# Gathering every second expert tile by quarters of a row and turning it on VectorE in squares of 32

## What is computed

```python
def _L0_ffn_ref(x, gate_W, gate_b, W1, b1, g1, be1, W2, b2, g2, be2):
    xf = x.reshape(BN, D)                       # 4096 x 512, already normalised
    gate_scores = xf @ gate_W + gate_b
    topk_scores, topk_idx = jax.lax.top_k(gate_scores, 2)
    weights = jax.nn.softmax(topk_scores, axis=-1)
    def expert(w1, bb1, gg1, bbe1, w2, bb2, gg2, bbe2):
        h = jax.nn.relu(_layernorm(xf @ w1 + bb1, gg1, bbe1))
        return _layernorm(h @ w2 + bb2, gg2, bbe2)
    all_out = jax.vmap(expert)(W1, b1, g1, be1, W2, b2, g2, be2)
    exp_out = all_out[topk_idx, jnp.arange(BN)[:, None]]
    return (jnp.sum(weights[..., None] * exp_out, axis=1) + xf).reshape(B, N, D)
```

## Time and profile before

| | |
|---|---|
| median of 3 runs | 1172.0 us (1169.74 to 1174.47) |
| profiled execution | 1170.26 us, its span 1168.5 us |
| granted TensorE clock, mean | 0.991 |
| busy: PE, PEld, DVE | 95%, 77%, 78% of the span |
| busy: ACT, POOL | 62%, 34% |
| DMA, mean | 124 GB/s |

### The profile page before, as it was taken

How to read it: one execution, slowest core, us unless ns; L and a number is a source line. 1 busy time by engine, 2 the same in 40 slices (tenths; PEclk the granted TensorE clock), 3 DMA queues, 4 the chain that set the end, 5 groups by cost and what they waited for, 6 DMA issues and landing times.

```text
span 1168.5 us, 24237 instructions
## 1 busy us (share of the span) xinstructions
PE 1108.3 (95%) x6017; PEld 905.0 (77%) x6018; DVE 910.5 (78%) x2172; ACT 722.2 (62%) x2148; POOL 393.4 (34%) x328
## 2 busy tenths in 40 slices
PE   6999999999989999999999888999999999999993
PEld 5888888888877787777777666777888888888882
DVE  6888888887874778878878877877777777777774
ACT  5223332233377777768676644866787787877873
POOL 3000000000034433545536364445534434443432
PEclk9999999999999999999999998999999999999998
DMA  8544545445340133143143377786555454444543
GB/s 261 163 149 159 190 148 173 151 163 207 126 147 1 57 89 111 56 124 100 46 145 90 128 206 219 201 249 152 94 85 81 81 85 80 86 81 81 88 63 40
DMA packets 95316, 144.76 MB, mean 124 GB/s; under 512 B 20864, under 2 KB 37428, under 8 KB 94607
## 3 DMA queue, kind: packets, MB, share of 16 engines
q1 hardware_dynamic: 77338, 106.83, 28.8%
q0 software_dynamic: 17216, 35.73, 17.4%
q10 hardware_dynamic: 693, 1.36, 0.4%
HBM read 82.69 MB, written 64.76 MB: 126 GB/s over the span
## 4 chain that ended last, share of the span: by engine, by line
PE 72%; DVE 9%; issue 7%; DMA 6%; ACT 3%; POOL 2%; DVEq 0%; POOLq 0%; ACTq 0%; SPq 0%
PE banks L1126 27%; PE banks L716 17%; PE banks L928 7%; PE banks L781 6%; DMA out<-rows,scatter_rows 4%; PE banks L893 3%; PE banks L906 3%; PE banks L1154 2%; PE banks L1138 2%; ACT rows L1335 2%; DVE operands L1615 2%; PE banks L917 1%; PE banks L754 1%; DVE rows L1917 1%; ACT operands L1218 1%
## 5 line engine op out<-in xcount | busy, mean ns | idle before, releaser
L1126 PE MATMUL banks<-operands 128*128 x1608 | 390.5, 398 | 9.2 <-ACT operands L1218 5.0
L1126 PEld LDWEIGHTS banks<-operands 128*128 128x128 f32 x1608 | 299.5, 190 | 73.9 <-issue 14.2
L716 PE MATMUL banks<-operands 128*128 128x512 f32 (+2 forms) x1224 | 290.1, 393 | 3.6 <-DVE operands L1615 3.6
L716 PEld LDWEIGHTS banks<-operands 128*128 128x128 f32 (+1 forms) x1224 | 226.1, 192 | 48.3 <-DVE operands L1615 3.7
L1218 ACT ACTIVATE operands<-banks 128x512 fp32r<-128x512 f32 (+1 forms) x232 | 137.6, 602 | 63.4 <-PE banks L807 34.2
L1615 DVE TENSOR_TENSOR operands<-banks,operands 128x512 fp32r<-128x512 f32 (+1 forms) x232 | 156.7, 683 | 15.6 <-ACT operands L1218 12.2
L1335 ACT ACTIVATE rows<-banks,score_shift 128x77 f32<-128x77 f32 x512 | 158.4, 337 | 11.2 <-DVE score_shift L1839 10.9
L2686 POOL DMA_INDIRECT out<-rows,scatter_rows x67 | 106.4, 1588 | 155.3 <-DVE rows L2419 109.7
L1218 ACT ACTIVATE operands<-rows 128x512 fp32r<-128x512 f32 (+2 forms) x77 | 54.0, 710 | 163.6 <-DVE rows L1686 139.4
L1540 ACT ACTIVATE banks<-banks,param_cols 128x128 f32<-128x128 f32 x268 | 99.2, 431 | 82.2 <-PE banks L1154 75.6
L2357 DVE BATCH_NORM_STATS2 moe_stats<-banks 128x6 f32<-128x512 f32 x134 | 93.2, 696 | 37.5 <-PE banks L1126 31.5
(11 more groups left out here) (191 smaller groups left out, 1603.1 us busy)
## 6 DMA issues: line engine op xcount, KB each, us to landing
expert_parts<-operands SPq DMA_DIRECT2D x32, 512.0 KB, 3.0
operands<-expert_parts SPq DMA_DIRECT2D x8, 2048.0 KB, 11.4
rows<-in_x SPq DMA_DIRECT2D x8, 1024.0 KB, 5.5
rows<-in_L_ffn_W SPq DMA_DIRECT2D x32, 256.0 KB, 3.6
x_rows<-rows SPq DMA_DIRECT2D x8, 1024.0 KB, 4.3
rows<-x_rows SPq DMA_DIRECT2D x8, 1024.0 KB, 6.2
xf_rows<-rows SPq DMA_DIRECT2D x32, 256.0 KB
out<-rows SPq DMA_DIRECT2D x32, 256.0 KB
```

Of the source, the lines that this page charges most:

```text
L716: last = nc.tensor.matmul(dst, stationary(a, k), moving(b, k), start=(t == 0 and k == 0), stop=(t == len(terms) - 1 and k == n_k - 1))
L1126: last = nc.tensor.matmul(dst, stationary[:, a, k, :], weights[:, w, bass.ds(e, 1), a2, k, :].rearrange("p e f -> p (e f)"), start=False, ...
```

## The change

The 27 tiles of even number from 14 on (`in_squares`) take another way from the table to xT:

- Their rows are read as four quarters of 128 features. An index now names a quarter of a row: token x 4 + quarter. Partition 32q + r of the buffer gets quarter q of four tokens, in four indirect DMAs of 128 pieces of 512 bytes. The first two go in GpSimd's turn of tile i-5, the other two in that of tile i-4.
- VectorE turns the buffer in 32x32 squares (`turn_rows`) at the start of the turn of tile i-3, from buffer `xg[0]` into `xq_turned` in SBUF. TensorE's four transposes of these tiles are gone. `rows_hi` and `rows_lo` read xq_turned.
- For the squares to come out with features on partitions, partition p holds features 4p to 4p+3. So W1's rows are loaded in that order for all tiles, and the transposes that stay on TensorE read every fourth element of the gathered rows.
- Each of these tiles has its slots loaded a second time in four pieces, one for each group of 32 partitions (`square_slots`), and the index is made by a scalar_tensor_tensor instead of a copy.
- In the turns with a `turn_rows`, ScalarE's square root goes behind the high part of the hidden rows.
- One semaphore for the transposed rows becomes two, and one wait at the start moves to another semaphore.

```diff
+SQUARES_FROM = 14
+SQUARES_N = SQUARES_FROM // 2
+        xf_quarters = xf_d.rearrange("t (q f) -> (t q) f", q=KC)
+        xq_rows = xg[0].rearrange("p (b f k) -> p b k f", b=P // SQ, k=KC)
+        xq_turned = f_at(60, KC * P)
+        xq_features = xq_turned.rearrange("p (k b r) -> p k r b", k=KC, b=P // SQ)
...
+        def in_squares(n, u):
+            return u == 0 and (not isinstance(n, int) or n >= SQUARES_N)
...
-                    src = io[name].rearrange("e (k p) f -> e k p f", p=P)
+                    src = io[name].rearrange("e (k p) f -> e k p f" if n // 2 else "e (p k) f -> e k p f", p=P)
...
+                if in_squares(n, u):
+                    for q in range(KC):
+                        sp.dma_start(square_slots[q * SQ:(q + 1) * SQ, bass.ds(n - SQUARES_N, 1)].rearrange(
+                            "p n b w -> p (n b w)"), slots_d[bass.ds(row, P), :].rearrange(
+                                "(r b) w -> r (b w)", r=SQ)).then_inc(slots_in[u], 16)
...
-                    last = nc.tensor.transpose(cx_bank[u][:, k * P:(k + 1) * P], xg[u][:, k * P:(k + 1) * P], ident[:, :])
-                last.then_inc(cx_done, 1)
+                    last = nc.tensor.transpose(cx_bank[u][:, k * P:(k + 1) * P],
+                                               xg[u].rearrange("p (f k) -> p k f", k=KC)[:, k], ident[:, :])
+                last.then_inc(cx_done[u], 1)
...
-                if after >= 3:
+                if after >= 3 and not in_squares(n + 1 + u, 1 - u):
                     rows_in(n + 1 + u, 1 - u)
...
+                if in_squares(n, u):
+                    hi_part(xT[:, HI].rearrange("p k (r b) -> p k r b", r=SQ), xq_features).then_inc(cx_hi, 1)
+                else:
+                    hi_part(xT[:, HI].rearrange("p k t -> p (k t)"), cx_bank[u]).then_inc(cx_hi, 1)
...
-                if after is not None and after >= 2:
+                if after is not None and after >= 2 and not behind:
                     deviations(i, True, True)
                 need(act, m2_done, i)
                 act.wait_ge(relu_done, KC * (i + 1))
                 hi_part(hTc[:, HI].rearrange("p k t -> p (k t)"), ch_bank).then_inc(hh_ready, 1)
+                if after is not None and after >= 2 and behind:
+                    deviations(i, True, True)
...
                 rows = slice(q * SQ, (q + 1) * SQ)
+                V.memset(quarter_ix[rows, 0, :], float(q))
...
+            def turn_rows(n):
+                dve.wait_ge(gathered[0], gathers(n + 1, 0))
+                need(dve, cx_lo, 2 * n - 1)
+                V.transpose(xq_turned.rearrange("p (k b r) -> p b k r", k=KC, r=SQ), xq_rows).then_inc(cx_done[0], 1)
...
+                if in_squares(n, u):
+                    V.scalar_tensor_tensor(
+                        gix_squares, square_slots[:, bass.ds(n - SQUARES_N, 1), :, 0].rearrange("p n b -> p (n b)"),
+                        float(KC), quarter, ALU.mult, ALU.add).then_inc(gix_ready, 1)
+                    return
...
+                if after >= 3 and in_squares(n + 1 + u, 1 - u):
+                    turn_rows(n + 1 + u)
...
+                if in_squares(n, u):
+                    for b in parts:
+                        G.indirect_dma_start(xg[0][:, b * P:(b + 1) * P], None, xf_quarters,
+                                             bass.IndirectOffsetOnAxis(gix_squares[:, b:b + 1], 0)).then_inc(
+                            gathered[u], 16)
+                    return
...
-                if after >= 5:
+                if u == 0 and after >= 4 and in_squares(n + 2, 0):
+                    gather(n + 2, 0, (2, 3))
+                if after >= 5 and in_squares(n + 2 + u, 1 - u):
+                    gather(n + 2 + u, 1 - u, (0, 1))
+                elif after >= 5:
                     gather(n + 2 + u, 1 - u)
```

75 lines of the change are left out of this document (44 added, 31 removed).

## The result

The change makes the kernel slower: 1194.0 us (median of 4 runs, 1191.7 to 1196.8) against 1172.2 in the same sitting, a ratio of 1.0194 with the 95% interval 1.017 to 1.0217. The profiled execution has a span of 1191.2 us for 1168.5. The forecast of 1166.0 and its range to 1177 are both missed.

What follows compares the result with a forecast made beforehand. The prediction took TensorE to bound the kernel. From the profiled 1170.3 us, -11.7 for removed transposes, +3.5 and +2.5 at the start and +1.5 for the later expert load gave 1166.0 us, range 1159 to 1177.

Steps and rivals of the forecast that it cites:

- worth 0.43 us: TensorE: removing one group of row transposes saves 0.43 us, 27 times, -11.7 us if nothing else comes to bind.
- Four transfers for one: GpSimd, steady part: the extra gathers add 3.9 us per two tiles, 10.3 of 12.25 us, so they fit.
- At the start it does not fit: GpSimd's early tiles: late second quarters for tile 14 cost +3.5 us, the overfull next three pairs +2.5.
- near 788: SyncE: added slot loads put the last expert load 5.4 us later, near 788, costing +1.5 us (bounds -2 and +4).
- Both hidden: Odd tile: square root behind the high part leaves the high part 0.25 us margin; the later low part is hidden too.
- 681 ns: VectorE: one 32x32 transpose of 128x512 per two tiles takes 681 ns, hidden with 0.35 us to spare per pair.
- the strided reads of the parts: VectorE and ScalarE: low and high parts keep about their old times, 0.63 and 0.69 us, at no cost.
- Rival 4: VectorE and ScalarE read slowly with a stride: +0.35 us on two instructions, 12.5 per pair, 1173 us; chance 0.05.
- The strided weight loads at nothing: TensorE: loading weights from every fourth fp32 in the 40 remaining groups costs nothing, 0 to 17 us kept open.
- Rival 2: TensorE's strided weight loads are slow, making the kernel slower than before: 1183 us if doubled; chance 0.14.
- Rival 1: No stall at the start, as quarters land in time or GpSimd is freed earlier: 1159 to 1161 us; chance 0.24.
- Rival 3: Second pair of quarters late in every pair: 0.3 us beyond VectorE's spare time, 8 us in all, 1174; chance 0.17.

Runs made afterwards that it cites:

- e11: e9 with VectorE's turn, the high part and the low part reading in order: 1166.8 us, ratio 0.994.
- e1: Changed kernel with no tile taken in squares, leaving only W1's new row order and the strided weight loads: 1173.3 us, ratio 0.999.
- e17: Kernel before plus two unread gathers per tile from 16 on, ahead of its own, 512-byte pieces from places 66 kB apart: 1212.5 us, ratio 1.035.
- e18: e17 with whole rows of 2 kB instead of 512-byte pieces: 1211.6 us, ratio 1.032.
- e9: Changed kernel with even tiles' rows gathered whole in one transfer; VectorE's turn and strided reads stay: 1172.0 us, ratio 0.999.
- e3: Changed kernel with VectorE's turn reading the gathered quarters in order: 1193.3 us, ratio 1.016.
- e4: e3 with the high and low parts also reading the turned buffer in order: 1193.7 us, ratio 1.017.
- e13: Kernel before plus one unread whole-row gather per tile from 16 on, right behind the tile's own: 1171.2 us, ratio 0.998.
- e16: Kernel before plus one unread whole-row gather ahead of each tile's own from 16 on, both behind the previous tile's finished rows: 1169.2 us, ratio 0.997.

## Why the prediction was wrong

- **One group "worth 0.43 us", -11.7 in all.** The price of a group was right, and TensorE's work did fall by it; what failed is "if nothing else comes to bind". Without the extra transfers and VectorE's and ScalarE's strided reads (e11) 0.19 a pair came out of it, 0.30 against e1.
- **"Four transfers for one ... 10.3 of 12.25. In the steady part that fits."** This step failed. It fits GpSimd's time and not the signals: the cost of a transfer was taken to be its issue and its landing. The runs show a third one, TensorE's signals late where gathers stand close together: by 0.8 us on average in the changed kernel, by up to 3.5 in e17 and e18. By e9 it is 9.0 of the 22 us. I had no row for it: between 900 and 1140 us the kernel before has no late signal. It has some, over 1 us late, before 725 us, in stages with other transfers, but no view that I read puts a semaphore's rise beside the instruction that raises it.
- **"At the start it does not fit", +3.5 and +2.5.** This step was too small. The mechanism was right, the size was not. The quarters' issue at 799.5 was as forecast, but the landing took 5.7 us after its end instead of 2.0, beside the last expert load (797.8, in flight to about 809), two more gathers and a slot scatter: VectorE waited 8.03 for the forecast's 4. The sum also put nothing for the clock, which was 0.50 for 10.2 us around that wait, some 2.8 us of TensorE's work. The pairs after it lost more than the 2.5 as well: by e9 the term is 12.4 at tile 22 instead of 6.0.
- **The last expert load "near 788", +1.5.** It went at 797.8, as L650 of the changed kernel shows:

```profile
L650 SPq DMA_DIRECT2D operands<-expert_parts x8: 55/408/755, 650.2 to 797.8; - x8
...
DMA to landing us min/median/max: 9.2/11.1/13.0
```

  15.6 us later than before and not 5.4; in e1, without any added slot load, it went at 788.0, so some 6 us of it can be one execution's chance. Its price seems to be within the bounds: e9, which has all the slot loads and the last expert load at 799.5, reaches tile 22 at 873.8, e1 at 873.4.
- **"Both hidden" on ScalarE, a margin of 0.25.** With the signals in time (e11) the second product waits 0.15, so the margin was short by 0.4 of what I took. With signals 0.6 late it was bound to fail.
- **VectorE's turn, "681 ns", and the strided reads of the parts, "nothing".** 1082 ns for the turn, 1.07 for the low part (0.69), 1.16 for the high part (0.61). Rival 4 had this mechanism at 12.5 a pair and 1173 in all; e9 measured 12.64 and 1172.0, the mechanism with a size somewhat larger, and the time partly by luck. In the changed kernel the signals lie above it.
- **The strided weight loads at nothing.** Close: 0.05 for a group, some 2 us over the kernel for e1. Rival 2 fell.
- **Rival 1** (no stall at the start) fell: the stall was larger than forecast. **Rival 3** (second pair late in every pair) fell too: the turn's waits end with the start (11.5 us in 3 waits, 3.3 in one).
- The signs: 160 transposes right; the turn's waits at the start right in place, in size not (8.0, 0, 3.3, 2.8 and 0.6 us in its first five turns for 4 and then 1 in each of three); tiles of 5.9 and 6.35 wrong (6.68 and 6.39), last expert load wrong, high and low part wrong (1.16 and 1.07 for 0.63 and 0.69). A steady pair over 12.4 us and a strided load over 150 ns were named as what would prove it wrong, and both came (13.09 us, 208 ns).

## What to carry to other kernels

Count gathers on GpSimd's queue not only in its own time: here two more in each tile (three in a row, from places far apart), though nobody waits for their data, cost over 3%, while one more cost nothing. The late signals went with three gathers that had a scatter-add close behind them. A long wait of TensorE was followed by some us at half clock: price it too. When an engine is idle in front of work whose input has been ready, compare the end of the producer with the rise of its semaphore before blaming either engine's work. And an experiment that removes a suspected cost under another bound shows nothing (e3, e4): take the upper bound away first (e9), then it shows (e11).

## Not expected of the hardware

- TensorE's semaphores normally rise 0.29 us (transposes) and 0.40 us (products) after the start of the instruction, and up to 3.5 us later than that in e17 and e18, with three gathers in a row; VectorE's and ScalarE's were never late beside them.
- A 32x32 turn of 128x512 fp32 takes 1.08 us when it reads every fourth element (16 bytes apart) and 0.70 in order (e4); reads 128 bytes apart cost VectorE 1.07 for 0.66 and ScalarE 1.16 for 0.63. TensorE's weight load from every fourth element takes 208 ns for 140, of which some 13 ns for each transpose came through (e1, 0.05 for a group).
- In the changed kernel TensorE's granted clock fell to 0.50 within its wait of 8.82 us and stayed there up to 817.6, 5.6 us past the wait's end; in e17 it fell at 1051.4, at the end of a wait of 2.57 us (0.65 on average from 1051.80 to the tile's end).
- A second gather of 128 pieces in each tile was free (e13 to e16, 1169.2 to 1171.2 beside 1172.6).
